# Key transposes and shifted-input transposes moved ahead in TensorE's order, with the key copy ahead in ScalarE's

## What is computed

```python
x = x + window_attention(layernorm(x), ...)          # 16 heads of 8, windows of 64
h = layernorm(x)
for i in range(6):
    h = attn_layer(shift_tokens(h), Wqkv[i], ...) + h   # 16 heads of 64, windows of 32 that also see the window before
    h = ffn_layer(shift_tokens(h), ...) + h             # layernorm, 128 -> 2 x 341, exact gelu gate, 341 -> 128
x = x + h
```

## Time and profile before

| | |
|---|---|
| median of 3 runs | 3424.12 us (3419.42 to 3426.51) |
| the profiled execution | 3419.42 us, its span 3417.6 us |
| mean granted TensorE clock | 0.978 of full |
| busy, share of the span | TensorE 93%, VectorE 82%, ScalarE 75%, GpSimd 77% |

### The profile page before, as it was taken

One profiled execution on the slowest core, in us unless ns is written; L12 is line 12 of the kernel. 1 busy time (PEld: TensorE's weight loads), 2 busy tenths in 40 slices (PEclk: granted clock), 3 DMA queues, 4 the chain that ended last, 5 costly groups with the idle time before them and its releaser, 6 DMA issues.

```text
span 3417.6 us, 126620 instructions
## 1 busy us (share of the span) xinstructions
PE 3167.5 (93%) x52802; PEld 2724.6 (80%) x52802; DVE 2817.6 (82%) x3743; ACT 2579.9 (75%) x3707; POOL 2625.9 (77%) x2593
## 2 busy tenths in 40 slices
PE   7968999989999989999989999989999998999996
PEld 4647888878788878888878878878888887888885
DVE  7967888888788888878888888888888888888883
ACT  6756778778778778877777778778777787787775
POOL 6658878778778878878778878787777887887872
PEclk9979999999999999999999999999999999999998
DMA  1001111111111111111101111111121111111111
GB/s 63 2 10 37 61 35 33 38 28 45 59 35 38 35 32 41 42 56 35 39 27 46 35 58 39 33 33 39 35 64 33 33 39 33 42 33 38 35 33 35
DMA packets 57802, 130.41 MB, mean 38 GB/s; under 512 B 10992, under 2 KB 33136, under 8 KB 56432
## 3 DMA queue, kind: packets, MB, share of 16 engines
q1 hardware_dynamic: 57200, 121.94, 12.3%
HBM read 19.17 MB, written 2.10 MB: 6 GB/s over the span
## 4 chain that ended last, share of the span: by engine, by line
PE 47%; DVE 21%; issue 15%; POOL 11%; ACT 5%; POOLq 0%; DVEq 0%; DMA 0%; ACTq 0%; SPq 0%
PE pair L211 38%; PE pair L214 9%; POOL qk L1062 5%; DVE ss L963 5%; DVE ts L959 5%; DVE pair L976 2%; DVE den L1011 2%; DVE qk L955 2%; ACT sq L819 2%; POOL Sx L1094 1%; POOL qk L1083 1%; DVE mx L980 1%; DVE Sx L984 1%; POOL rnt L1099 1%; POOL rn L1108 1%
## 5 line engine op out<-in xcount | busy, mean ns | idle before, releaser
L1083 POOL TENSOR_TENSOR qk<-qk,ts 128x1024 f32<-128x1024 f32 x384 | 911.1, 2384 | 224.8 <-DVE ts L959 211.0
L955 DVE TENSOR_TENSOR qk<-pair,tab 128x1024 f32<-128x1024 f32 x384 | 468.3, 1220 | 364.0 <-ACT sq L819 361.3
L1062 POOL TENSOR_TENSOR qk<-qk,rn 128x1024 f32<-128x1024 f32 x384 | 733.2, 1931 | 26.6 <-issue 11.5
L211 PE MATMUL pair<-wq_h,xs_h 128*128 128x512 f32 x1154 | 515.2, 447 | 34.9 <-issue 16.4
L814 ACT ACTIVATE Sx<-Sx 128x1024 f32<-128x1024 f32 x192 | 203.4, 1060 | 412.4 <-DVE Sx L984 412.4
L1094 POOL TENSOR_TENSOR Sx<-Sx,rden 128x1024 f32<-128x1024 f32 x192 | 365.4, 1903 | 159.3 <-DVE rden L1014 159.3
L959 DVE TENSOR_TENSOR ts<-pair,tab 128x1024 f32<-128x1024 f32 x384 | 466.0, 1213 | 0.0
L211 PE MATMUL pair<-wq_h,xs_l 128*128 128x512 f32 x1152 | 464.7, 403 | 0.2
L963 DVE TENSOR_REDUCE ss<-sq 128x16 f32<-128x1024 f32 x384 | 464.1, 1209 | 0.0
L214 PEld LDWEIGHTS pair<-small,qk 128*128 128x128 f32 x3104 | 357.3, 144 | 131.7 <-POOL qk L1062 52.0
L211 PE MATMUL pair<-wq_l,xs_h 128*128 128x512 f32 x1152 | 461.8, 401 | 0.5 <-issue 0.5
(11 more groups left out here) (126 smaller groups left out, 6668.8 us busy)
## 6 DMA issues: line engine op xcount, KB each, us to landing
VB<-VA SPq DMA_DIRECT2D x192, 384.0 KB, 3.5
VB<-VA SPq DMA_DIRECT2D x96, 128.0 KB, 3.5
wq_raw<-wqkv SPq DMA_DIRECT2D x6, 1536.0 KB, 7.4
xf<-xT SPq DMA_DIRECT2D x96, 64.0 KB, 1.9
xf<-xT SPq DMA_DIRECT2D x96, 63.8 KB, 2.0
wo_sb<-wo SPq DMA_DIRECT2D x6, 512.0 KB, 4.2
X<-x_in SPq DMA_DIRECT2D x4, 512.0 KB, 7.7
out<-X SPq DMA_DIRECT2D x8, 256.0 KB, 2.3
```

What stands on the lines that cost most here:

```text
L211: return T_.matmul(out, lhsT, rhs, start=start, stop=stop, **k)
L955: V_.tensor_tensor(h3(qk[:, now, kind, :], DH), h3(source[:, :], DH), rep(tab[:, 2 * kind, b, :], HEADS, DH), ALU.mult)
L1062: G_.tensor_tensor(x, x, bc(rn[:, then, kind * HEADS:(kind + 1) * HEADS], HEADS, DH), ALU.mult).then_inc(S["scaled"], 1)
L1083: G_.tensor_tensor(qk[:, now, kind, :], qk[:, now, kind, :], ts[:, kind, :], ALU.add).then_inc(S["added"], 1)
```

## The change

Three groups of instructions change their place in an engine's order; none is added or taken away, and every wait goes with its group.

1. TensorE: kT (with its waits) now stands between AV and V; it stood behind V.
2. TensorE: in odd steps the two transposes of `xf` now stand ahead of w2 and of the turning back; they stood behind both.
3. ScalarE: the copy of kT now stands ahead of the copy of V; it stood behind it.

```diff
@@ step_pe
                 last.then_inc(S["av_done"], 1)
-            if pl.has(0):
-                e.wait_ge(S["rotated"], blocks(pl, "rotated", 0, 1))
-                if fresh:
-                    e.wait_ge(S["wq_low_v"], layers(pl, 1, t // NBLOCKS, 1))
-                project(one, high, low, 2 * INNER).then_inc(S["v_done"], 1)
             if pl.has(1):
                 e.wait_ge(S["scaled"], blocks(pl, "scaled", 1, 2))
                 e.wait_ge(S["qkT_kept"], blocks(pl, "qkT_kept", 1, 1))
                 for a in range(PAIRS):
                     last = tr(PC[:, a * P:(a + 1) * P], qk[:, then, 1, a * P:(a + 1) * P])
                 last.then_inc(S["qkT_done"], 1)
+            if pl.has(0):
+                e.wait_ge(S["rotated"], blocks(pl, "rotated", 0, 1))
+                if fresh:
+                    e.wait_ge(S["wq_low_v"], layers(pl, 1, t // NBLOCKS, 1))
+                project(one, high, low, 2 * INNER).then_inc(S["v_done"], 1)
...
+            q = pl.seq(5)
+            if q is not None:
+                e.wait_ge(S[f"xf{q % 2}"], pl.times(SEQS // 2 * 32) + (q // 2 + 1) * 32)
+                if pl.has(1):
+                    e.wait_ge(S["qkT_kept"], blocks(pl, "qkT_kept", 1, 2))
+                elif pl.seq(11) is not None:
+                    e.wait_ge(S["gated"], seqs(pl, "gated", pl.seq(11), 3))
+                for h in range(BLOCKS):
+                    last = tr(bank2[:, h * P:(h + 1) * P], xf[:, q % 2, h * P:(h + 1) * P])
+                last.then_inc(S["turned"], 1)
             q = pl.seq(11)
...
                 last.then_inc(S["turned_back"], 1)
-            q = pl.seq(5)
...
@@ step_act
+            if pl.has(1):
+                e.wait_ge(S["qkT_done"], blocks(pl, "qkT_done", 1, 2))
+                bb = (t - 1) % BLOCKS
+                A_.activation(kT[:, :, WIN + bb * P:WIN + (bb + 1) * P], h3(PC[:, :], P), ACT.Copy).then_inc(S["qkT_kept"], 1)
             if pl.has(0):
                 e.wait_ge(S["v_done"], blocks(pl, "v_done", 0, 1))
...
                 A_.activation(VA[:, r, :], one[:, :], ACT.Copy).then_inc(S["v_kept"], 1)
-            if pl.has(1):
...
```

More of the change, by code:

```diff
@@ L766, in step_pe @@
                 last.then_inc(S["turned_back"], 1)
-            q = pl.seq(5)
-            if q is not None:
-                e.wait_ge(S[f"xf{q % 2}"], pl.times(SEQS // 2 * 32) + (q // 2 + 1) * 32)
-                if pl.has(1):
[L771 to L776, removed]
             if pl.has(1):
@@ L850, in step_act @@
                 A_.activation(VA[:, r, :], one[:, :], ACT.Copy).then_inc(S["v_kept"], 1)
[L851 to L854, removed]
             q = pl.seq(9)
```

## The result

The changed kernel takes 3449.63 us (median of 4 runs, 3446.21 to 3455.97), the kernel before, run beside it, 3425.32. The ratio is 1.0066, with a 95% interval of 1.0047 to 1.0086: 0.7% slower, 24.3 us. The forecast was 3443 us, 19 us above before, in a range of 3428 to 3462. The profiled execution of the changed kernel took 3445.39 us with a span of 3443.6, 26.0 more than the span before.

What follows compares the result with a forecast made beforehand. TensorE's order from pT to the scores was taken to bound even steps, with slack in odd ones. 72 even steps at 0.32 us, less 4.0 gained at the start, gave 19.0 us more: 3443 us, range 3428 to 3462.

Steps and rivals of the forecast that it cites:

- kT ahead of V: TensorE behind AV: kT must wait for ScalarE's query copies, starting 0.14 us behind them; w1 starts 0.32 us late.
- The even step's price: Even steps, where TensorE has no slack before `mx`: each pays 0.32 us, between 0.21 and 0.42.
- 72 x 0.32: Even steps where AV is not held up, times the lateness of each: 23.0 us in all.
- The odd step: Odd steps: the same lateness meets slack of 0.76 us at `mx` and 0.30 at pT; costed at nothing.
- The rival that odd steps pay too: Hand-over 0.10 us longer, so odd steps add 12 us and even ones 30: 3462 us; chance 0.10.
- Kept copies swapped: ScalarE in even steps: table load, gelu and gating 0.19 us late, arriving together with the scores; nothing added to 0.32.
- The gain at the start: First pipeline steps without w1: VectorE's idling for the scores, 4.3 us in nine places, shrinks; 4 us taken as gained.
- xf ahead of w2, "price nothing": Odd steps on TensorE: no new wait and later w2 harmless, so no cost; without V's cover, a few tenths each.
- The sum: Whole kernel: 23.0 us less 4.0 gives 19.0 us slower, 3443 us on the median.
- low bound of 0.21: Least lateness of w1 per even step, in us, if the hand-over to kT is as short as 0.06.
- TensorE has room: Rival: TensorE takes the wait in and VectorE's chain binds; no change, about 3420 to 3426 us; chance 0.12.
- The stalls in AV shrink: Rival: up to 46.3 us of unexplained AV idle time come back, 3397 us at best, deciding above 26; chance 0.08.

Runs made afterwards that it cites:

- V split: Against the kernel before: kT between the two halves of V, its copy ahead of V's on ScalarE, xf at its old place; 3417.57 us, ratio 0.9996.
- xf-only run: Change 2 alone against the kernel before: xf ahead of w2 and the turning back, V still ahead of kT; 3519.33 us, ratio 1.0293.
- keys only: Changes 1 and 3 without change 2, against the kernel before; 3425.98 us, ratio 1.0027; once more in another series 3432.73 us, ratio 1.0025.
- keys with xf early at the end alone: Changes 1 and 3, xf ahead of w2 only in steps that project no block, against the kernel before; 3433.23 us, ratio 1.0028.
- first series: Runs on one chip beside the kernel before (3417.29 us): the change's parts by themselves, xf late at the end only, and V in halves around kT.

## Why the prediction was right, and where its sum was not

**kT ahead of V: right.** kT starts 0.14 us behind the copies, as read from the pair pT and qT, and w1 is 0.32 us late, as worked out. Shown by experiment: without the wait the pair is 30.84 us, with half of V ahead of it 30.94, with the wait 31.12.

**The even step's price: mis-sized.** The term "72 x 0.32" took w1's lateness as that of the scores. From w1's start to the scores it was 2.34 us and is 2.24, since w1 now follows a projection and not the transposes (2.22 with V split, where it follows a projection too), and the scores are only 0.22 late. The regular pair grew by 0.22 us in the mean over 44 pairs. The count was too high as well. In the trace before, V starts about 1.9 us behind L837 in 67 of the 91 even steps, not 72; and the 25 held-up pairs at full clock grew by only 0.02 us each in the mean, so there the later scores cost next to nothing.

**The odd step: right.** In the median odd step `mx` starts 0.53 us behind the scores' end instead of 0.77, still held by VectorE. The rival that odd steps pay too is out. The xf-only run shows the other side: a delay of 1.5 us there breaks through.

**Kept copies swapped: right.** The table load is 0.19 us late, as forecast. Gating ends at 1732.42 and the scores at 1732.37, so both chains reach `mx` at about the same time in the changed kernel too. The traces do say which holds it. Where gating holds it, `mx` starts 0.07 to 0.08 us ahead of gating's recorded end: in 91 of 92 even steps with the copies swapped alone, 0.81 to 0.84 behind the scores, and in 89 with V split, 0.10 to 0.16 behind them. In the kernel before it starts 0.05 us behind the scores in all 92 (the last, at 3342.04, comes after the 91 that the prediction counted), while its distance from gating's end changes from step to step; in the changed kernel this is so in 87. There the scores hold it, and VectorE has 0.15 us or less to spare in nearly all of these steps. The Trainium skill's page "PSUM — Partial Sum Buffer", section "Summary: rules for kernel authors", says to evacuate promptly. The copy order by itself costs 1.9% here: prompt for kT means late for V on an engine that works in order.

**The gain at the start: a part of it.** The five waits for the key copy, 6.0 us, are gone, but 2.5 us came of it where 4.0 were counted. The prediction put all nine places where VectorE idles for the scores into the first steps. In the trace three of them (0.84 us) lie at 1520, 2431 and 2582. The first, 1.15 us at the first scored block, stays as it is, and the 0.41 at the second becomes 0.63. Only four go, of 0.47 each. Those four steps come out 0.6 us shorter each.

**xf ahead of w2, "price nothing": the step that failed.** It was right that there is no new wait in the steady steps and the regular pair is the same 31.12 us. It missed the last layer, where `xf` is loaded from what its own step has just written: 3.0 us of waiting instead of 1.15 with w2 behind it, in all profiles with xf early there. And in the loop xf's new place costs 10.5 and 8.8 us, in two series. It doesn't show in regular pairs, and the mean clock is the same. What goes with it is AV's unnamed idle time: 36.5 and 38.3 us with keys only, 44.6 and 49.9 with xf moved in the loop as well. That is the size of the difference, but this sum differs between executions of one kernel too (50.5 and 44.1), and the 45.0 of keys with xf early at the end alone come from an execution that was itself 10 us slower than the median. So that the place in the loop costs is shown by two pairs of runs; that it does so through AV is not shown, and the cause is open. The last section tells what these stops in AV go with.

**The sum.** Keys alone were measured at 8 to 9 us. By the measured terms the regular pairs' 9.5 less 2.5 give 7, and 72 even steps at 0.22 less 2.5 would give 13: the held-up pairs pay less than was counted. The forecast of 19 for the whole change, against 24.3 and 27.3 measured, is close by luck in its parts: a price too high in the key part stood in for an xf part that was missing. (The low bound of 0.21 leaves out the prediction's own 0.03 for a start out of a wait; with it, it is 0.24.)

**The rivals.** "TensorE has room" is out: weight loads are busy for 26.55 of 31.12 us, so by the rule of the Trainium skill's page "Perfetto Trace Analysis", section "Identifying the Most-Contended Engine", there would still be 15% of room, and yet 0.2 us of waiting in an even step shows in full. "The stalls in AV shrink" came true to a small part in keys only, by 8 to 10 us of the 26 that it needed, little more than two executions of one kernel differ by, and not in the whole change.

No version beats the kernel before: the best that computes everything, V split around kT, is level with it.

## What to carry to other kernels

Before work is moved ahead on an in-order engine, look at what still holds its buffer at the new place; what stood there was perhaps the cover. Find the hand-over whose distance stays constant over all steps: in undisturbed steps a delay that reaches it costs in full, and beside a slack of 0.76 us a delay of 0.27 is free where one of 1.5 is not. Price a move in the last steps of a pipeline separately, since a transfer that had three steps of time in the middle has none there.

## What the runs showed that was not expected

At the kernel's end, where TensorE waits between short bursts, its clock made more of a difference than the moved work. The same 26 matmul records took 7.17 us at a granted clock of 1.00 and 10.55 at 0.50; over all profiles but that of the run with kT ahead of AV, the last stretch took from 67.6 to 75.4 us with xf late and from 70.8 to 77.4 with xf early. In the run with kT ahead of AV the mean clock was 0.846 against 0.978.

In a stream of 64 small matmuls TensorE stands still for about one microsecond at a time with no wait that the profile names, 33 to 51 us per kernel (10.9 in the run with kT ahead of AV). With the same matmuls in all kernels the sum differs between kernels, and by 6 us between two executions of one.

The packets of the trace show what these stops go with. The page lists a queue of its own for instructions (before: q8, 432 packets, 7.08 MB, so 16 KB each). Around one stop in the kernel before, the DMA view of 482.20:482.30 and the timeline of TensorE from 484 on:

```profile
q8 instruction: 1, 0.02, 54.8%
```

```profile
484.69 0.25 PE L211 MATMUL pair<-PT,VB 64*64 64x32 f32 x3 [0.99 <-issue]
```

The packet starts at 482.28 and takes 0.88 us, to 483.15; TensorE goes on 1.54 us behind its end. It is so each time: the 14 profiles have 567 stops of over 0.4 us in AV, and all of them end 1.19 to 1.60 us behind the end of a q8 packet. In each of the steps with such a stop the packet starts between 0.45 us ahead of AV's start and 1.05 behind it; of the 2121 steps without one, only 572 have a packet there. So TensorE seems to wait for its next instructions when a packet is asked for in the densest part of the step. No run moved a packet by itself, so this is a reading of the traces and not an experiment.

A stop is at times paid twice. In the kernel before, nine short stretches at a granted clock of 0.50 lie in the loop outside the layers' starts, and each begins 0.1 to 1.4 us behind a stop in AV of 1.0 to 1.5 us. Of the 13 pairs whose lengths differ by over 1.3 us between the two traces, 12 have such a stretch in one of them or both. The time of one kernel goes with its mean clock from run to run: of the 27 runs of the kernel before in the first series, the three at 0.978 and 0.979 took 3409.87 to 3411.75 us and the one at 0.971 took 3427.79, the longest.
